# Constant operand rows filled on chip, operand parts stored as they are made, later slot zeroing, a loop written out, and weight tiles of two experts, in a transformer and mixture-of-experts kernel

## The chip, the core and the metric

The kernel runs on one core of a Trainium2 chip. Its engines are TensorE (PE, with a weight load PEld that overlaps the matmuls), VectorE (DVE), ScalarE (ACT), GpSimd (POOL) and SyncE (SP, which here only issues DMAs). A "q" behind an engine's name (SPq, PEldq) is its sequencer: the part that reads instructions, computes registers, waits on semaphores and issues DMAs. The metric is the device time of one execution in microseconds, lower is better.

## The reference

The input x has 2 batches of 512 tokens of 128 values. Two layers follow, each `x = x + ffn(cond(x))`:

- Layer 0, cond: attention of 16 heads of 8 values. Q, K and V come from x by `c_attn_w` and `c_attn_b`; a key and a value of an image row (from `cond_1024`, `uk`, `uv`) stand ahead of the 512 others; the scores are causal, an additive mask row is added, softmax, then the values and `c_proj`.
- Layer 0, ffn: eight experts; each token goes to the two with the highest score and takes the mean of their outputs. An expert is 128 to 512 (W1), gelu, 512 to 512 (W2), gelu, 512 to 128 (W3).
- Layer 1, cond: a product with a weight that `cond_1024` scales and norms. Layer 1, ffn: a two-matrix expert layer with top-2 routing and a capacity of 320 tokens an expert.

## The kernel before

**Attention operands.** Scores are made in bf16 with the precision of float32: Q and K are each cut into three bf16 parts (high, middle, low), and the products that matter are summed over six rows per head dimension, 48 rows in all. Three rows more carry the mask (ones in Q, mask parts in K) and three the negated row maximum (maxima in Q, ones in K). ACT and DVE make the parts of Q and K of a batch `b` into `part` (lines 743, 745, 1285, 1291). SP stores them in DRAM as `q_rows[b]` and `k_rows[b]`, [64 rows, 16 heads, tokens], one DMA for each group of 8 rows (`store_parts`, L463), beside ten DMAs of constant rows (L472 to L480, from `mrowone` and `mrowzero`) and six of mask rows (L485). Then it loads them back by groups of four heads into one of four slots of `qr` and `kr` (`load_rows`, L500 and L501), which POOL has filled with zeros (L639). Everything of this stands in the order of SP's queue: constants, mask, parts of batch 0, loads of groups 0 and 1, parts of batch 1, loads of groups 2 and 3, maxima.

**Attention.** There are eight groups n (two batches of four). A first pass (`score`, L948 and L950, and the reduction L1416 on DVE) gives the row maxima; DVE copies them, transposed, to `mrow` (L1427), and SP puts them in `qr` (`store_max`, L507). A second pass (`second_scores`, L962 and L968) gives exponents (ACT, L784), and `values` (L990) the outputs. An order written out by hand (`schedule`) merges the first pass of group n with the second pass of group n - 2, so the second pass of group 0 comes right after the first two score pieces of group 2.

**Expert weights of layer 0.** 24 tiles of 512 KB go through a ring of four (`w_ring`, loads issued by POOL, L645); ACT makes the high f16 part (`high_part`, L760), DVE the low one (`low_part`, L1357). They stand at fixed places of the schedule: nine sparse, the rest two score units apart near its end. A W2 tile is 128 rows by 128 columns of all eight experts, so its runs in DRAM are 512 bytes. `x0_slots` (4.1 MB), `x1_slots` and `y_rows` (2.3 MB) are zeroed by four DMAs of ACT's queue (L736), whose source is a zeroed weight buffer.

**Expert layer 0.** 23 blocks of 128 tokens. Block i on PE: `second_layer(i)` (12 matmuls of 512 columns, L1093), `first_layer(i+2)` (L1081), `transpose_x(i+3)` (L1070), `transpose_z(i)` (L1104), `third_layer(i-1)` (L1115). ACT has `gelu1(i+2)` and `gelu2(i)` (L796), DVE the copies and splits, SP the loads of tokens. The expert of a block is a value in a table in SBUF; `table` (L412) loads it into registers of an engine (TENSOR_LOAD). Three blocks are written out, then four iterations of a loop of four blocks (`Fori`, L1139 on PE) with one load for seven values on PE (six on ACT, four on DVE and SP), then four blocks written out again with one load. Layer 1 follows.

## Time and profile before

| | us |
|---|---|
| three runs: median (lowest to highest) | 462.86 (460.72 to 464.38) |
| the profiled execution | 464.21 |
| its span | 462.4 |
| mean granted clock of PE, as a share of 2.4 GHz | 0.828 |

| engine | busy us | share of the span | instructions |
|---|---|---|---|
| PE | 313.4 | 68% | 2480 |
| PEld | 189.5 | 41% | 2495 |
| DVE | 282.1 | 61% | 719 |
| ACT | 176.4 | 38% | 405 |
| POOL | 135.5 | 29% | 161 |

The span is one execution on the chip. Busy shares are averages over stages with different limits: which engine or DMA ends the wait in a stage has to be read there. "issue" as a releaser means that the engine waited for nothing that the profile shows, so its own sequencer was late. By stage: operands of attention 0 to 50 us, attention to 204, routing and transition to 225, the blocks of expert layer 0 to 352, layer 1 to the end.

### The profile page before, as it was taken

The page shows a single profiled execution, that of the slowest core. Times are in us where ns is not written, and L with a number is a line of the kernel's source. Part 1 is how long each engine was busy: PE and PEld are TensorE (multiplying, and loading weights), DVE is VectorE, ACT ScalarE, POOL GpSimd, SP SyncE. Part 2 cuts the span into 40 slices and gives each one's busy share as a digit, 9 for nine tenths or more (in the row PEclk, how much of TensorE's full clock was granted, in tenths as well). Part 3 has the DMA queues.
Part 4 walks back from the last instruction along what each step waited for, and adds up shares of the span by engine and source line. Part 5 has one row for each costly group of instructions (what it writes and reads, how often), then busy time and mean ns, then how long its engine had stood idle before and what let it go on. Part 6 is the DMA issues. An engine that isn't in the chain of part 4 may idle for free.

```text
span 462.4 us, 8035 instructions
## 1 busy us (share of the span) xinstructions
PE 313.4 (68%) x2480; PEld 189.5 (41%) x2495; DVE 282.1 (61%) x719; ACT 176.4 (38%) x405; POOL 135.5 (29%) x161
## 2 busy tenths in 40 slices
PE   4550447999987777446579797989894436577820
PEld 2440223444444322225256555645552423365620
DVE  4870463888887755356875656655666683474623
...
GB/s 264 291 212 146 233 251 29 50 130 127 118 74 53 15 232 265 100 41 47 119 83 180 130 21 24 23 28 17 23 13 12 98 29 51 69 30 62 38 43 139
DMA packets 24802, 45.21 MB, mean 98 GB/s; under 512 B 4098, under 2 KB 14930, under 8 KB 24644
## 3 DMA queue, kind: packets, MB, share of 16 engines
...
## 4 chain that ended last, share of the span: by engine, by line
PE 42%; DVE 15%; issue 13%; DMA 10%; SPq 10%; another core or an unknown queue 5%; ACT 3%; POOL 2%; ACTq 0%; DVEq 0%; POOLq 0%
PE pair L1093 15%; PE bank L990 4%; SPq L463 3%; DMA k_rows<-part 3%; PE bank L1104 3%; PE bank L968 2%; PE bank L1115 2%; DMA w_ring<-in_L_ffn_W_dram 2%; PE pair L1081 2%; PE pair L948 2%; DMA qr<-mrow 2%; PE bank L982 2%; SPq L485 2%; DMA back<-y_rows 2%
## 5 line engine op out<-in xcount | busy, mean ns | idle before, releaser
L1093 PE MATMUL pair<-w_sb,h 128*128 x276 | 68.1, 400 | 16.5 <-issue 9.4
L1416 DVE TENSOR_REDUCE mA<-pair 128x2 f32<-128x256 f32 (+3 forms) x64 | 50.9, 820 | 36.9 <-PE pair L950 36.3
L645 POOL DMA_DIRECT2D w_ring<-in_L_ffn_W_dram x24 | 21.5, 897 | 140.8 <-DVE w_sb L1357 108.7
L796 ACT ACTIVATE h<-pair,cols 128x128 f32<-128x128 f32 x92 | 26.2, 368 | 92.2 <-PE pair L1081 70.9
L784 ACT ACTIVATE p_ring<-bank 128x512 f32<-128x512 f32 (+1 forms) x88 | 45.9, 562 | 34.5 <-PE bank L971 34.4
L948 PE MATMUL pair<-kr,qr 128*128 128x128 bf16 (+3 forms) x122 | 32.8, 323 | 25.5 <-DMA kr<-k_rows 21.0
...
L1093 PEld LDWEIGHTS pair<-w_sb,h 128*128 128x128 f16 x276 | 26.3, 102 | 49.6 <-issue 23.9
L660 POOL DMA_INDIRECT x_slots<-sent,slot x32 | 31.1, 971 | 40.1 <-DVE slot L1671 16.7
L968 PE MATMUL bank<-qr,kr 128*128 128x384 bf16 (+3 forms) x120 | 33.4, 322 | 5.8 <-ACT p_ring L784 5.6
L948 PEld LDWEIGHTS pair<-kr,qr 128*128 128x128 bf16 x128 | 13.2, 105 | 47.8 <-issue 31.3
L1357 DVE SCALAR_TENSOR_TENSOR w_sb<-w_ring,w_sb 128x1024 f16<-128x1024 f32 x22 | 26.7, 1219 | 7.4 <-ACT w_sb L760 7.3
L1530 DVE COPY z<-pair 128x512 f32<-128x512 f32 x23 | 15.9, 691 | 24.6 <-PE pair L1093 24.6
L796 ACT ACTIVATE h<-bank,cols 128x128 f32<-128x128 f32 x92 | 26.6, 394 | 7.2 <-PE bank L1104 7.2
L950 PE MATMUL pair<-causal_a,identb 128*128 128x128 bf16 x128 | 27.7, 235 | 1.1 <-DVE mA L1416 0.8
L760 ACT ACTIVATE w_sb<-w_ring 128x1024 f16<-128x1024 f32 x22 | 23.2, 1057 | 12.5 <-PE pair L1022 9.6
L971 PE MATMUL bank<-causal_b,identb 128*128 128x128 bf16 x128 | 26.3, 232 | 1.1 <-issue 0.8
L990 PE MATMUL bank<-p_ring,v_sb 128*9 128x512 f32 (+3 forms) x256 | 24.7, 459 | 0.7 <-ACT p_ring L784 0.5
L1230 PE MATMUL bank<-w_sb,hT 128*128 128x128 f16 (+1 forms) x288 | 20.9, 229 | 4.8 <-issue 3.2
L777 ACT ACTIVATE pimg<-bank 128x512 f32<-128x512 f32 x8 | 4.8, 598 | 47.2 <-PE bank L962 47.2
L968 PEld LDWEIGHTS bank<-qr,kr 128*128 128x128 bf16 x128 | 13.0, 102 | 23.2 <-ACT p_ring L784 12.0
L1230 PEld LDWEIGHTS bank<-w_sb,hT 128*128 128x128 f16 (+1 forms) x288 | 18.2, 107 | 8.5 <-issue 4.4
...
## 6 DMA issues: line engine op xcount, KB each, us to landing
...
```

The lines of the kernel that those rows point to most:

```text
L660: pool.indirect_dma_start(dst, bass.IndirectOffsetOnAxis(ap=slots[:, k, b, r:r + 1], axis=0), row.bitcast(F16) if dst is x0_d else row, No ...
L784: act.activation(p_ring[:, w % P_RING, 0:width], bank(4 + v % 3)[:, 0:width], ACT.Exp).then_inc(exp_done, 1)
L796: ins = act.activation(to[:, c * P:(c + 1) * P], got[:, c * P:(c + 1) * P], ACT.Gelu, bias=cols[:, bass.ds(e * HC + (bias_row + c), 1)], s ...
L948: mm(to[:, 0:n_keys], qr[:, n % SLOTS, j, t * P:(t + 1) * P], kr[:, n % SLOTS, j, IMG:IMG + n_keys], start=True, stop=False)
L950: ins = mm(to[:, t * P:n_keys], identb[:, :], causal_a[:, :], start=False, stop=True)
L968: mm(to[:, i * width:(i + 1) * width], kr[:, n % SLOTS, j0 + i, IMG + kc * P:IMG + (kc + 1) * P], qr[:, n % SLOTS, j0 + i, kc * P:], start ...
L971: ins = mm(to[:, i * width:i * width + P], identb[:, :], causal_b[:, :], start=False, stop=True, skip_group_check=True)
L990: ins = mm(bank(7)[32 * j:32 * j + HD + 1, kc * P:], v_sb[:, b, kc, g * G + j, :], p_ring[:, w % P_RING, i * width:(i + 1) * width], start ...
L1093: ins = mm(bank(3), h1[:, s, hq, k * P:(k + 1) * P], w2_sb[k][wq][:, bass.ds(e * HID, HID)], start=(k == 0 and n == 0), stop=(k == HC - 1 ...
L1230: ins = mm(bank(4 + e % 2)[0:k, t * P:t * P + D], hT[:, e % 2, hq, c, t * P:t * P + k], cp16[wq][:, e, c * D:(c + 1) * D], start=(c == 0 a ...
L1357: dve.scalar_tensor_tensor(out=lo, in0=w_ring[n % W_RING][:, :, :], scalar=W_UP, in1=hi, op0=ALU.mult, op1=ALU.subtract).then_inc(w_lo, 1)
L1416: dve.tensor_reduce(mA[:, b, t, g * G + 2 * hp:g * G + 2 * hp + 2], got[:, :, 0:(t + 1) * P], AX_X, ALU.max).then_inc(a_used, 1)
```

## The change

- The constant rows are no longer stored in DRAM and loaded again. ACT fills all of `qr` and `kr` (an activation of a zero column with a bias that holds ones in rows 64 to 66 or 96 to 98); POOL clears a few columns of `kr` behind it. The mask parts go straight to `kr`. DRAM keeps 48 rows, and a slot's load has 48 rows. For groups 4 to 7, whose slots are used again, SP issues four DMAs more for each (three of mask, one of zero maxima).
- Head channels are put in the order (dimension, head), by ACT copies of the weight columns (`wqk`) and of three rows (`rows_own`), so that a stored part is one DMA over all partitions; each part is stored as soon as it is made, in copies, three DMAs each for Q and K of a batch instead of six. PE waits for both copies (`wqk_ready`, `own_ready`).
- Seven small loads move from ACT's queue to SP's. The zeroing of `x0_slots` moves from ACT's queue to POOL's, behind the first four weight tiles. That of the other two stands behind ACT's fills.
- W2 and W1 tiles are two experts by 128 rows by 512 columns: runs of 2048 bytes. W3 is as before.
- The blocks of expert layer 0 are written out; each engine loads one value a block. PE has 19 loads instead of 6, ACT 19 instead of 6, DVE 21 instead of 5, SP 20 instead of 5.

The core of the diff (names and renamed arguments that only follow are left out):

```diff
-Q_PART = (0, 0, 1, 1, 0, 2)
-K_PART = (0, 1, 0, 1, 2, 0)
-PROD_ROWS = len(Q_PART) * HD
-MASK_ROW = PROD_ROWS
-MAX_ROW = MASK_ROW + 3
-ZERO_ROW = MAX_ROW + 3
-ROWS = 64
+Q_PART = (0, 0, 0, 1, 1, 2)
+K_PART = (0, 1, 2, 0, 1, 0)
+ROWS = len(Q_PART) * HD
+MASK_ROW = 64
+MAX_ROW = 96
 SLOTS = 4
+ONES2 = 1.0 + 16256 / 2 ** 23
...
+            k, two = divmod(n, HC)
+            pair_of = slice(2 * two, 2 * two + 2)
+            in_pair = lambda t: t[:, 2 * two * HID:(2 * two + 2) * HID]
             if n < HC * HC:
-                k, m = divmod(n, HC)
-                return W2[:, cols_of(k), cols_of(m)], [by_expert(t, cols_of(m)) for t in w2_sb[k]]
-            k = (n - HC * HC) % HC
+                return (W2[pair_of, k * P:(k + 1) * P, :].rearrange("e p n -> p e n"),
+                        [in_pair(t) for t in w2_sb[k]])
             if n < HC * HC + HC:
-                return W1[:, :, cols_of(k)], [by_expert(t, cols_of(0)) for t in w1_sb[k]]
-            return W3[:, cols_of(k), :], [by_expert(t, cols_of(0)) for t in w3_sb[k]]
+                return W1[pair_of].rearrange("e p n -> p e n"), [in_pair(t) for t in w1_all]
+            k = two
+            return W3[:, k * P:(k + 1) * P, :].rearrange("e p n -> p e n"), [t[:, :] for t in w3_sb[k]]
...
+            for to, source, signal in (
+                    (vb_bc[:, :], attn_b[2 * D:3 * D].partition_broadcast(P), misc_in),
...
+                    rows = (k_rows_d if i else q_rows_d)[b].rearrange("(c d) h t -> (d h) c t", d=HD)
+                    width = IMG + S if i else S
+
+                    def store(first, last, m, copies):
+                        src = part[:, n, m:m + last - first, 0:width] if copies == 1 else (
+                            part[:, n, m:m + 1, 0:width].broadcast_to([P, copies, width]))
+                        sp.dma_start(rows[:, first:last], src).then_inc(rows_out[n], 16)
+
+                    sp.wait_ge(hi_ready, n + 1)
+                    store(*((5, 6, 0, 1) if i else (0, 3, 0, 3)))
+                    sp.wait_ge(act_step, n + 1)
+                    store(*((3, 5, 0, 1) if i else (3, 5, 1, 2)))
                     sp.wait_ge(parts_ready, n + 1)
-                    rows, which = (k_rows_d[b], K_PART) if i else (q_rows_d[b], Q_PART)
-                    width = IMG + S if i else S
-                    for c, m in enumerate(which):
-                        sp.dma_start(rows[c * HD:(c + 1) * HD].rearrange("d h t -> h d t"),
-                                     part[:, n, m, 0:width]).then_inc(rows_out[n], 16)
...
-                sp.dma_start(k_rows_d[b][MASK_ROW:MAX_ROW, :, 0:IMG].rearrange("r h t -> h r t"),
-                             zero_rows_of(3, IMG)).then_inc(krest_out[b], 16)
-            sp.wait_ge(mask_ready, 1)
-            for b in range(B):
+                    store(*((0, 3, 0, 1) if i else (5, 6, 2, 1)))
+
+            def load_mask(b, first, last, signal):
+
                 for m in range(3):
-                    sp.dma_start(k_rows_d[b][MASK_ROW + m:MASK_ROW + m + 1, :, IMG:],
-                                 mpart[b:b + 1, m:m + 1, :].broadcast_to([1, H, S])
-                                 ).then_inc(krest_out[b], 16)
+                    sp.dma_start(kr[MASK_ROW + m:MASK_ROW + m + 1, first:last, :, IMG:].rearrange("p s j t -> p (s j) t"),
+                                 mpart[b:b + 1, m:m + 1, :].broadcast_to([1, (last - first) * G, S])
+                                 ).then_inc(signal, 16)
...
                 if n >= SLOTS:
                     sp.wait_ge(s_done, s_index(n - SLOTS + 1, 0))
+                    load_mask(b, n % SLOTS, n % SLOTS + 1, qk_in[n % SLOTS])
+                    sp.dma_start(qr[MAX_ROW:MAX_ROW + 3, n % SLOTS],
+                                 zero_row[:, :].rearrange("p (o t) -> p o t", o=1).broadcast_to([3, G, S])
+                                 ).then_inc(qk_in[n % SLOTS], 16)
...
             store_parts(0)
+            sp.wait_ge(filled, 2)
+            sp.wait_ge(trimmed, 1)
+            sp.wait_ge(mask_ready, 1)
+            load_mask(0, 0, SLOTS, masked)
             rows_stored(0)
-            sp.wait_ge(padded, 1)
             load_rows(0)
             load_rows(1)
...
-            for t in (qr, kr):
-                ins = pool.memset(t[:, :, :, :].bitcast(U32), 0)
-            ins.then_inc(padded, 1)
+            pool.wait_ge(filled, 2)
+            pool.memset(kr[MAX_ROW:MAX_ROW + 3, :, :, 1:IMG], 0.0).then_inc(trimmed, 1)
...
             pool.wait_ge(qk_in[1], 32)
             for n in range(W_RING):
                 load_weights(n)
+            x0_clear = x0_d.rearrange("(h p n w) c -> h p n (w c)", h=2, p=P, w=CLEAR_RUN)
+            run = CLEAR_RUN * (2 * D + 2)
+            for h in range(2):
+                pool.dma_start(x0_clear[h], zeros[:, 0:run].rearrange("p (o c) -> p o c", o=1).broadcast_to(
+                    [P, x0_clear.shape[2], run])).then_inc(zero0_out, 16)
...
+            act.wait_ge(fill_ready, 1)
+            for t, col in ((qr, 1), (kr, 2)):
+                flat = t[:, :, :, :].rearrange("p s j t -> p (s j t)").bitcast(F32)
+                act.activation(flat, fill[:, 0:1].broadcast_to([P, flat.shape[1]]), ACT.Identity,
+                               bias=fill[:, col:col + 1]).then_inc(filled, 1)
+                if col == 1:
+                    act.wait_ge(wqkv_in, 16)
+                    act.copy(wqk[:, :, :].rearrange("p i (d h) -> p i d h", h=H),
+                             wqkv[:, 0:2 * D].rearrange("p (i h d) -> p i d h", i=2, d=HD)).then_inc(wqk_ready, 1)
+            act.wait_ge(rows_in, 16 * 9)
+            own = slice(ROW_QK, ROW_UK + 1)
+            act.copy(rows_own[own, :].rearrange("p (d h) -> p d h", h=H), by_dim(rows_sb[own, :])).then_inc(own_ready, 1)
+
             x1_clear = x1_d[0:DUMP1].rearrange("(p n w) d -> p n (w d)", p=P, n=4)
             y1_clear = y1_d[1:FREE1].rearrange("(p n w) d -> p n (w d)", p=P, n=1)
             act.wait_ge(zeroed, 1)
             act.wait_ge(x_in, 16)
-            for target in (x0_clear[0], x0_clear[1], x1_clear, y1_clear):
+            for target in (x1_clear, y1_clear):
...
+            own = slice(ROW_QK, ROW_UK + 1)
+            pe.wait_ge(own_ready, 1)
+            tr(bank(2)[:, own], rows_own[own, :], ident[own, own])
             tr(bank(2)[:, P:2 * P], uk_sb, ident[:, :])
             tr(bank(2)[:, 2 * P:3 * P], uv_sb, ident[:, :]).then_inc(cols_done, 1)
             pe.wait_ge(xT_ready, 1)
-            pe.wait_ge(wqkv_in, 16)
-            mm(bank(4), wqkv[:, 0:D], xT[:, 0, :], start=True, stop=True).then_inc(qkv_done, 1)
-            mm(bank(5), wqkv[:, D:2 * D], xT[:, 0, :], start=True, stop=True).then_inc(qkv_done, 1)
+            pe.wait_ge(wqk_ready, 1)
...
+            first_layer(1, 1)
             pe.wait_ge(tab_ready, 1)
-            of = table(mybir.EngineType.PE, 0, 0, LEAD + 2)
-            for i in range(LEAD):
-                second_layer(0, i, of[i])
-                first_layer(0, i + 2, of[i + 2])
-                transpose_x(0, i + 3)
-                transpose_z(0, i)
+            of = list(table(mybir.EngineType.PE, 0, 0, LEAD + 2))
+            for i in range(NB):
+                second_layer(i, of[i])
+                if i + 3 < NB and i + 3 >= len(of):
+                    of += table(mybir.EngineType.PE, 0, i + 3, 1)
+                if i + 2 < NB:
+                    first_layer(i + 2, of[i + 2])
+                if i + 3 < NB:
+                    transpose_x(i + 3)
+                transpose_z(i)
                 if i == 0:
                     pe.wait_ge(w_lo, W_TILES - W3_POOL)
                     pe.wait_ge(w_lo_pool, W3_POOL)
                 if i:
-                    third_layer(0, i - 1, of[i - 1])
-            with pe.Fori(0, LOOPS) as j:
-                of = table(mybir.EngineType.PE, 0, UNROLL * j + (LEAD - 1), UNROLL + 3)
-                for n in range(UNROLL):
-                    second_layer(j, LEAD + n, of[n + 1])
-                    first_layer(j, LEAD + n + 2, of[n + 3])
-                    transpose_x(j, LEAD + n + 3)
-                    transpose_z(j, LEAD + n)
-                    third_layer(j, LEAD + n - 1, of[n])
-            of = table(mybir.EngineType.PE, 0, REST - 1, NB - REST + 1)
-            for i in range(REST, NB):
-                second_layer(0, i, of[i + 1 - REST])
-                if i + 2 < NB:
-                    first_layer(0, i + 2, of[i + 3 - REST])
-                if i + 3 < NB:
-                    transpose_x(0, i + 3)
-                transpose_z(0, i)
-                third_layer(0, i - 1, of[i - REST])
-            third_layer(0, NB - 1, of[NB - REST])
+                    third_layer(i - 1, of[i - 1])
+            third_layer(NB - 1, of[NB - 1])
...
+            of = list(range(LEAD - 1))
+            for i in range(NB):
+                if i == LEAD - 1:
+                    dve.wait_ge(lead_in, 16 * LEAD)
+                    copy(id_all[:, LEAD - 1:LEAD], xg_lead[:, LEAD - 1, 2 * D:].bitcast(I32)).then_inc(id_copied, 1)
+                    dve.wait_ge(id_copied, 1)
+                copy_z(i)
+                if i >= len(of):
+                    of += table(mybir.EngineType.DVE, 0, i, 1)
+                if i + 3 < NB:
+                    copy_x(i + 3)
+                if i + 2 < NB:
+                    split_1(i + 2)
```

**SP's queue where the operands of batch 0 are stored.** Before, between the second batch's constants and the load of group 0 (`part` is the cut operand, `mpart` the cut mask):

```order
L472 DMA q_rows<-mrowone 16x3x512
L474 DMA q_rows<-mrowzero 16x13x512
L476 DMA k_rows<-mrowone 16x3x544
L478 DMA k_rows<-mrowzero 16x10x544
L480 DMA k_rows<-mrowzero 16x3x32
L485 DMA k_rows<-mpart 16x1x512 x6
L463 DMA q_rows<-part 16x8x512 x6
L463 DMA k_rows<-part 16x8x544 x6
L500 DMA qr<-q_rows 64x2048
L501 DMA kr<-k_rows 64x2176
```

and in the changed program, from the last small input load on:

```order
L461 DMA gate_sb<-in_L_ffn_gate_w_dram 128x8
L473 DMA q_rows<-part 128x3x512
L473 DMA q_rows<-part 128x2x512
L473 DMA q_rows<-part 128x512
L473 DMA k_rows<-part 128x544
L473 DMA k_rows<-part 128x2x544
L473 DMA k_rows<-part 128x3x544
L485 DMA kr<-mpart 1x16x512 x3
L503 DMA qr<-q_rows 48x2048
L504 DMA kr<-k_rows 48x2176
```

28 DMAs (ten constants, six of mask, twelve parts) stood ahead of the first load of a slot; now nine do.

**ACT's start in the changed program** (before, ten input loads and four zeroing DMAs stood ahead of its first cast):

```order
L725 DMA wqkv<-in_L_cond_c_attn_w_dram 128x384
L726 DMA uk<-in_L_cond_uk_w_dram 128x128
L727 DMA uv<-in_L_cond_uv_w_dram 128x128
L732 ACT_TABLE_LOAD
L732 ACTIVATE qr<-fill 128x4096
L736 COPY wqk<-wqkv 128x256
L732 ACTIVATE kr<-fill 128x4352
L740 COPY rows_own<-rows_sb 3x128
L748 DMA x_slots<-w_sb 512x1x645
L748 DMA y_rows<-w_sb 128x2048
L756 CAST part<-q 128x512
```

Both fills stand ahead of the copy that PE waits for.

**PE in the blocks of expert layer 0.** Before, at the start of an iteration of four blocks:

```order
L1115 MATMUL bank<-w_sb,h 128x128
L1139 UNCONDITIONAL_BRANCH
L1139 ISA
L412 TENSOR_LOAD tab
L1088 REGISTER_ALU
L1090 REGISTER_ALU
L1093 ISA
L1093 MATMUL pair<-w_sb,h 128x512 x2
```

Now, in every block from the third to the twentieth (L1105 is `second_layer`, L1093 `first_layer`):

```order
L1105 REGISTER_ALU
L1105 MATMUL pair<-w_sb,h 128x512
L409 TENSOR_LOAD tab
L1093 ISA
L1093 MATMUL pair<-xgT,w_sb 128x128 x2
```

The load has moved from behind the short matmuls of `third_layer` to behind the long ones of `second_layer`, and has one value instead of seven.

## Rows read from the trace of the kernel before

**Rows 1.** The chain of waits, 0 to 51 us: start us, us, what.
```profile
16.69 2.33 SPq L472
...
42.69 2.44 DMA k_rows<-part
```

**Rows 2.** The timeline, 0 to 48 us: start us, us, engine, operation, [idle before <-releaser].
```profile
9.18 1.92 PE L897 MATMUL bank<-xT,wqkv 128*128 128x512 f32 x2
...
13.89 3.50 POOL L639 MEMSET qr<- 128x4096 uint32 x1
...
15.08 6.02 DVE L1304 TENSOR_SCALAR kimg_bd<-hmask,k 128x16 f32<-128x16 f32 x2
...
21.29 0.73 DVE L1273 TENSOR_SCALAR q<-bank,cols 128x512 f32<-128x512 f32 x1
...
34.00 0.42 DVE L1350 COPY wcT_sb<-pair 128x256 f32<-128x256 f32 x1 [0.58 <-PE pair L932]
...
45.72 0.60 SPq L501 DMA_DIRECT2D kr<-k_rows  x1
```

**Rows 3.** Groups of ACT instructions with shapes: count, busy us, mean ns, idle before.
```profile
L760 ACT ACTIVATE w_sb<-w_ring 128x1024 f16<-128x1024 f32 x22 | 23.2, 1057 | 12.5 <-PE pair L1022 9.6 <-DMA w_ring<-in_L_ffn_W_dram 2.8
...
L743 ACT ACT_TABLE_LOAD x1 | 1.3, 1283 | 10.3 <-issue 10.3
```

**Rows 4.** The timeline, 50 to 74 us.
```profile
50.50 0.26 PE L948 MATMUL pair<-kr,qr 128*128 128x128 bf16 x1 [16.54 <-DMA kr<-k_rows]
...
61.40 0.41 DVE L1427 COPY mrow<-pair 12x512 bf16<-12x512 bf16 x1
...
69.46 0.27 PE L948 MATMUL pair<-kr,qr 128*128 128x128 bf16 x1 [4.43 <-DMA kr<-k_rows]
...
73.08 0.62 PE L962 MATMUL bank<-qr,kr 128*32 128x512 bf16 x4 [3.03 <-DMA qr<-mrow]
```

**Rows 5.** The chain of waits, 65 to 73 us.
```profile
65.78 7.25 DMA qr<-mrow
```

**Rows 6.** Stretches: busy us (x) of PE, PEld, DVE, ACT, POOL; PEclk, DMA share, GB/s.
```profile
12.00:30.00 18.00, 9.97 (x48) 8.04 (x47) 15.27 (x27) 4.67 (x8) 8.91 (x5) 0.72 1.02 292
56.00:70.00 14.00, 7.05 (x44) 3.45 (x44) 9.72 (x18) 0.00 (x0) 1.04 (x2) 0.79 1.00 229
```

**Rows 7.** Who waited for whom, 140 to 225 us: us, times, longest.
```profile
ACT w_sb L760 <- DMA w_ring<-in_L_ffn_W_dram: 2.8, 2, 2.6
```

**Rows 8.** The chain of waits, 257 to 333 us.
```profile
257.33 2.68 PE pair L1093 x12
...
271.01 2.76 PE pair L1093 x12
...
275.88 2.72 PE pair L1093 x12
...
326.01 2.68 PE pair L1093 x12
...
332.30 2.76 PE pair L1093 x12
```

**Rows 9.** Single instructions of lines 412 and 1076: count, ns min/median/max, first start us.
```profile
L412 PEldq TENSOR_LOAD <-tab x1: 777/777/777, 224.0 to 224.0; - x1
...
L412 PEldq TENSOR_LOAD <-tab x1: 1711/1711/1711, 262.4 to 262.4; - x1
...
L412 ACTq TENSOR_LOAD <-tab x1: 908/908/908, 330.7 to 330.7; - x1
...
L1076 PEldq ALU_OP  x1: 32/32/32, 258.1 to 258.1; - x1
```

**Rows 10.** A stretch behind a loop boundary; columns as in Rows 6.
```profile
264.50:269.20 4.70, 4.70 (x21) 2.12 (x21) 0.29 (x1) 0.00 (x0) 0.81 (x1) 0.64 0.04 14
```

**Rows 11.** The timeline, one PE and one ACT row of the loop.
```profile
264.47 4.31 PE L1093 MATMUL pair<-w_sb,h 128*128 x12 [2.35 <-issue]
...
330.51 1.16 ACT L796 ACTIVATE h<-bank,cols 128x128 f32<-128x128 f32 x4
```

273 lines of the change are left out of this document (114 added, 159 removed).

## The prediction

> **What bounds the kernel now.** I went from the page's strip of 40 slices, which shows PE nearly idle in the first tenth, to the chain of waits. From 10 to 43 us it is one thing: SP issuing DMAs, each constant taking some 2.3 us to issue, and then the last stored part landing 2.44 us after its issue [rows 1]. SP and not the data is late: Q of batch 1 is computed at 21.3 us, and the last result that PE needs for its first score is copied at 34.0 to 34.4 us [rows 2]. Yet the first score starts at 50.50 us, after 16.54 us of idle time that a load of `kr` ends. Then PE works for 14.5 us, waits 4.43 us for the slot of group 2 and, two score pieces on, 3.03 us for the maxima of group 0, so the second pass starts at 73.08 us [rows 4]. Those maxima were ready at 61.8 us; the last of their DMAs took 7.25 us to land [rows 5], in a stretch in which the DMA engines were busy all the time at 229 GB/s [rows 6]. From there to the end of attention PE leads, but for 2.8 us that ACT waits for weight tiles [rows 7]. In the expert blocks PE leads too: a block takes 275.88 - 271.01 = 4.87 us [rows 8].
>
> **The first score.** The sum is against the profiled execution, 464.2 us, which is 1.3 us over the median shown; I leave that difference alone.
>
> ACT now starts with a table load of 1.28 us and two fills. From 1.06 us for 1024 elements [rows 3] 4096 and 4352 elements are an estimated 3.6 to 4.2 and 3.8 to 4.5 us. With the three DMA issues ahead (to about 2.3 us) and the two copies (0.7 us together) PE gets `rows_own` at about 12.5 us; behind it stand three transposes, so the first QK matmul starts near 13.1 us instead of 9.18 [rows 2]: 3.9 us later. Against that, POOL's fills go. Two products of 16 columns took 6.02 us on DVE while POOL filled `qr` and `kr` [rows 2]; the work behind them slipped from an estimated 17.6 us (their plain lengths added) to 21.29 us, 3.7 us. The two cancel to +0.2 us: PE is ready near 34.7 us.
>
> The other path is SP's. The last part of K of batch 0 is made at about 23.3 us (22.7 us before, the same shifts). Its store covers three copies: 1 us of issue and, from 2.44 us for a third of its bytes, 3 to 4 us of landing: 27 to 28 us; three mask DMAs lie beside it. The load of group 0 then took from 45.72 to 50.50 us, 4.8 us [rows 2, 4]: 33.5 us. Or by traffic: 2.3 MB of zeroing and 1.6 MB of parts at 229 to 292 GB/s [rows 6] are 13 to 17 us from 13 us on, thus 26 to 30, and the load at 31 to 36. I take 36 us for the first score, the later end, since the zeroing overlaps the stores. It cannot be before 34.7. The upper bound is that SP goes on issuing at 2.3 us each: nine DMAs from 16.6 us are 37.3, two loads 42, and with landing 44.5 us.
>
> **The second pass.** From the first score, PE needs 14.5 + 0.6 = 15.1 us of work to the second pass, thus 51.1 us. The maxima are ready 11.3 us after the first score, as before: 47.3 us; three issues at 0.6 us [rows 2], then landing, between 2.44 us [rows 1] and 7.25 us [rows 5]: 51.5 to 56.4 us. What speaks for the upper end is that 4.1 MB of zeroing now stand on POOL's queue right behind 2 MB of weights; against it, that before the maxima stood behind 1 MB of slot loads in their own queue, which now are 0.8 MB and issued some 12 us ahead of them. I take 53.5 us: **-19.6 us**, between -23 (49.9, all at its best) and -9 (44.5 + 15.1, and 4 us for the maxima).
>
> SP's four further DMAs for each of groups 4 to 7 cost 2.4 us of its queue, at 0.6 us each; a slot is free a group of work (12 us, nearly all of it PE's) ahead of its use and its load took 4.8, so they lie beside PE's work: 0, and if that cover were gone 4 x 2.4 us. POOL's clearing of a few columns of `kr` and the moved input loads lie ahead of 16 us on queues that wait: 0.
>
> **Weight tiles.** The runs of 2 KB can shorten a load; ACT's and DVE's part has the same 1024 elements, and its pace of two exponents and one high part (1.9 us a tile) sets the dense stretch. So at most the 2.8 us of [rows 7] is to be had, at least nothing: **-1.5 us**.
>
> **The blocks.** A loop boundary takes 264.47 - 257.33 = 7.14 us instead of 4.87 [rows 8, 11]: 2.27 us, four times; the boundary at the loop's exit 332.30 - 326.01 = 6.29, thus 1.42 [rows 8]. Together **-10.5 us**. PE's idle time there is marked as its own issue [rows 11], and the register load fills it: 1.71 us for seven values [rows 9]. Behind this boundary the granted clock was 0.64 of full speed, thus mostly the lower of the two levels, 1.2 GHz [rows 10]; the block took 271.01 - 264.47 = 6.54 us, 1.67 over, and one more behind another boundary about the same. These I count as gone with the idle time that precedes them: **-3.5 us**, at worst 0.
>
> What is added is a load in 18 blocks. At 258.1 us PE's sequencer had issued all of `second_layer` and was at the next register operation [rows 9], while those matmuls ran until 257.33 + 2.68 = 260.01 us [rows 8]: it is 1.9 us ahead. The new load stands in exactly this place. Its length for one value no row shows; five values on an idle PE took 0.78 us, seven 1.71 [rows 9], so I take 0.8 us as the nearest and 1.71 as the bound. With some 0.3 us of waits and register operations behind it, 1.1 us is hidden and even 1.9 nearly. That a load runs beside queued work is seen on ACT: one of 0.91 us from 330.7 [rows 9] while four activations ran from 330.51 to 331.67 us [rows 11]. ACT's `gelu2` may start 0.4 us later; what it feeds has over 1 us to spare. I add **+1 us** in all for such remains.
>
> The DMA page of the Trainium skill ("DMA: Bandwidth & Descriptors", section "Latency and other measured facts") speaks against this part: it gives a register load a floor of some 600 ns and says that the compiler unrolls by four to spread it. By that rule alone, all loads exposed, the time would be that of the second rival; the trace's 0.78 us for five values agrees with the floor, and only the place decides.
>
> **Sum.** 464.2 - 19.6 - 1.5 - 10.5 - 3.5 + 1.0 = 430.1: I predict **430 us**, with 422 to 437 for this case by itself.
>
> **The rivals.**
>
> 1. *The DMAs stay late.* SP's issues stay slow while the zeroing runs, or the maxima sit behind it; the second pass starts at 60 to 64 us and the gain is 9 to 13 instead of 19.6. For it: three small DMAs took 7.25 us under such traffic [rows 5]; against: two thirds of the zeroing is gone from that time. 437 to 441 us. Chance 0.14.
> 2. *The register loads are exposed*, on PE or by way of ACT or DVE: 18 x 0.6 to 0.8 us is 11 to 14 us, less the 1 us counted: 440 to 443 us. Against it stands the run-ahead of 1.9 us. Chance 0.12. Both together, about 452 us: 0.03.
> 3. *Slower than before*: PE's load waits until the array is empty and each block pays what a boundary paid. PE idled 2.35 us there [rows 11]; 18 times is 42 us, and the low clock behind two of five such gaps adds 18 x 0.4 x 1.7 = 12 us: 430.1 - 1 + 54 = 483 us. It makes the kernel slower from (464.2 - 429) / 18 = 2.0 us a block on. Against it: one value instead of seven and no branch. Chance 0.04.
> 4. *No difference*: the earlier start is given back in attention, since maxima, weights and slot loads share DMA queues with 4.1 MB more in that time, and the blocks win only part. Attention's 131 us from the second pass on would have to grow by 15 us or more; PE leads there. About 460 us, chance 0.03.
> 5. *More than summed*: the first score at 34.7 us and PE at the high clock level near attention's end. 415 to 421 us, chance 0.03.
>
> **The numbers.** The forecast has 0.61. The range 419 to 446 us leaves out rivals 3 to 5 and half of the double case, and part of the forecast's own spread, which makes 2 in 10 by a generous count of what I can't see. A measurement of this kernel can tell about 1% (4.6 us) from no change. Faster by more: the forecast, rivals 1, 2, 5 and the double case, 0.93. Within: 0.03. Slower: 0.04.
>
> **What would show it.** The first score at 35 to 37 us, its wait ended by a load of `kr` or by the copy of `wcT`, no DVE instruction of 6 us near 15 to 21 us; the second pass at 51 to 56 us; the first QK matmul near 13 us; blocks of 4.8 to 5.0 us throughout with no gap on PE before `first_layer`, and loads of 0.6 to 0.9 us; the blocks in about 114 instead of 127 us. The prediction is wrong if the maxima land after 57 us, if PE idles behind each load, or if the clock level falls inside the blocks.

## The result, and the profile after

| | before | after |
|---|---|---|
| median of the runs of this comparison (lowest to highest), us | 463.62 (460.72 to 467.16) | 426.06 (418.98 to 427.67) |
| ratio, 95% interval | | 0.909 (0.894 to 0.924) |
| the profiled execution, its span, us | 464.21, 462.4 | 418.98, 417.2 |

The change makes the kernel 8 to 9% faster; 430 us were forecast, with a range of 419 to 446. Ratios, here and below, are of the runs within 1.5% of the fastest of their kernel (418.98 and 424.34 us of six runs of the changed one), and the medians of the table alone would give 0.919. The profiled execution of the changed kernel is the shortest of its runs, 7 us under the median, so a sum over its stages gives more than the medians do. Its granted clock was 0.870, that of the other five 0.840 to 0.847.

The first reading is the start. These are rows of the changed kernel's timeline, the answer to [rows 2, 4] (start, length, engine, line and operation, idle time before and what ended it):

```profile
12.17 0.26 PE L902 MATMUL pair<-ident,rows_own 3*128 3x3 f32 x1 [4.23 <-ACT rows_own L740]
...
12.84 1.92 PE L907 MATMUL bank<-xT,wqk 128*128 128x512 f32 x2
...
18.17 0.37 DVE L1304 TENSOR_SCALAR kimg_bd<-head_of,k 128x16 f32<-128x16 f32 x2
...
25.03 0.42 SPq L504 DMA_DIRECT2D kr<-k_rows  x1
...
31.60 3.13 POOL L648 DMA_DIRECT2D w_ring<-in_L_ffn_W_dram  x4 [17.92 <-DMA kr<-k_rows]
...
33.41 0.42 DVE L1350 COPY wcT_sb<-pair 128x256 f32<-128x256 f32 x1 [0.59 <-PE pair L942]
...
34.07 0.27 PE L960 MATMUL pair<-kr,qr 128*128 128x128 bf16 x1 [0.70 <-issue]
...
51.79 0.40 PE L974 MATMUL bank<-qr,kr 128*32 128x512 bf16 x4 [2.43 <-DMA qr<-mrow]
```

PE waits 4.23 us for the copy of three rows that stands behind ACT's fill of `kr`. The two products that took 6.02 us on DVE beside POOL's fills take 0.37. Before, five DVE instructions that began between 15.08 and 17.09 us all ended between 21.09 and 21.37, when POOL's second fill ended (21.05): they stood still more than they ran slowly. SP issues the load of `kr` for group 0 at 25.03 us instead of 45.72, and POOL's row at 31.60 shows a load of `kr` as landed (it waits for group 1). The first score starts 0.66 us after the copy of `wcT` does, and its releaser is "issue", no load: the preparation on PE and DVE is late now, SP is not. It comes at 34.07 us instead of 50.50, and the second pass at 51.79 instead of 73.08. Of what still stands before that one, the chain of waits says:

```profile
46.98 4.76 DMA qr<-mrow
```

This answers to the 7.25 us of [rows 5]. And the stretches that answer to [rows 6] (us, then busy us of PE, PEld, DVE, ACT and POOL, the granted clock, DMA share, GB/s):

```profile
12.00:30.00 18.00, 12.67 (x57) 9.56 (x57) 12.98 (x32) 5.47 (x10) 1.63 (x2) 0.88 0.71 203
36.00:50.00 14.00, 9.18 (x61) 4.24 (x59) 12.73 (x22) 0.00 (x0) 0.23 (x1) 0.88 1.02 319
```

From 12 to 30 us the DMA engines now move 203 GB/s instead of 292; from 36 to 50 us they are full at 319 GB/s, with weights and the zeroing of `x0_slots` beside the maxima.

The second reading is the blocks. The chain of waits has `second_layer` of three blocks in a row, and one register load of PE follows it in the view of its line (count, ns least, median, most, first and last start):

```profile
242.67 2.71 PE pair L1105 x12
...
247.49 2.65 PE pair L1105 x12
...
252.25 2.69 PE pair L1105 x12
```

```profile
L409 PEldq TENSOR_LOAD <-tab x1: 301/301/301, 243.5 to 243.5; - x1
```

From the third on, a block takes 4.76 to 4.89 us, 4.80 in the mean; the load of one value takes 0.30 us, and no idle time stands behind it. Boundaries of 7.14 us [rows 8, 11] are gone, and so is the lower clock behind them [rows 10]. In the first two blocks it is not: `second_layer` takes 4.17 us in block 0 of this profile and 4.64 in block 1 of the second one.

Two pairs of profiles by stage, in us; "again" is a second profile of each kernel, from two later jobs in which the kernel before takes 452 and 454 us:

| stage, from the start of | before | after | before, again | after, again |
|---|---|---|---|---|
| the program, to the second pass | 73.08 | 51.79 | 71.99 | 53.10 |
| the second pass, to group 7 | 97.67 | 96.23 | 98.28 | 95.76 |
| group 7, to the first block | 54.45 | 45.44 | 42.81 | 40.49 |
| the first block, to the last `third_layer`'s end | 129.55 | 114.39 | 137.74 | 119.14 |
| layer 1, to the end | 107.70 | 109.38 | 98.06 | 99.32 |
| span | 462.4 | 417.2 | 448.9 | 407.8 |

The border at the first block is a soft one. Where that block starts early, PE waits in block 0, for its first tokens and for DVE: in the changed kernel the first block starts at 193.46 and 189.35 us, the third at 204.11 and 204.56.

### The profile page after: what moved, and what is told of

The parts are those of the page before. It is cut to its first block, busy times and chain, and to the rows that moved or that the text cites. A ratio compares the mean times of both kernels' runs of the same rounds, so it can differ in the third digit from the quotient of the medians.

```text
span 417.2 us, 7917 instructions
## 1 busy us (share of the span) xinstructions
PE 306.3 (73%) x2495; PEld 188.8 (45%) x2495; DVE 276.5 (66%) x719; ACT 185.4 (44%) x408; POOL 125.7 (30%) x163
## 3 DMA queue, kind: packets, MB, share of 16 engines
q0 software_dynamic: 8336, 26.47, 19.6%
## 4 chain that ended last, share of the span: by engine, by line
PE 55%; DVE 17%; issue 10%; DMA 6%; ACT 6%; POOL 2%; SPq 1%; another core or an unknown queue 1%; ACTq 1%; POOLq 0%; DVEq 0%
PE pair L1105 14%; PE bank L1002 4%; PE bank L1228 4%; PE bank L1115 4%; PE bank L1126 4%; PE pair L960 3%; DVE mA L1416 3%; PE pair L1093 3%; PE bank L980 3%; PE bank L994 2%; PE pair L1216 2%; ACT p_ring L798 2%; DMA y_rows<-y_sb,id_now 2%; POOL y_rows L718 2%; PE pair L1196 2%
## 5 line engine op out<-in xcount | busy, mean ns | idle before, releaser
L1105 PE MATMUL pair<-w_sb,h 128*128 x276 | 64.7, 385 | 3.9 <-DVE h L1539 3.9
L648 POOL DMA_DIRECT2D w_ring<-in_L_ffn_W_dram x24 | 18.3, 762 | 126.2 <-DVE w_sb L1357 108.3
L668 POOL DMA_INDIRECT x_slots<-sent,slot x32 | 31.7, 990 | 34.1 <-DVE slot L1659 17.2
L1105 PEld LDWEIGHTS pair<-w_sb,h 128*128 128x128 f16 x276 | 25.8, 99 | 33.9 <-issue 6.0
L980 PE MATMUL bank<-qr,kr 128*128 128x512 bf16 (+3 forms) x128 | 34.7, 317 | 5.8 <-ACT p_ring L798 5.6
L960 PE MATMUL pair<-kr,qr 128*128 128x128 bf16 (+3 forms) x128 | 33.7, 320 | 6.7 <-DVE mA L1416 5.7
L1228 PE MATMUL bank<-w_sb,hT 128*128 128x128 f16 (+1 forms) x288 | 22.0, 237 | 7.7 <-issue 5.7
L983 PE MATMUL bank<-causal_b,identb 128*128 128x128 bf16 x128 | 25.2, 225 | 0.0
L1710 DVE SCALAR_TENSOR_TENSOR hT<-w_sb,hT 128x640 f16<-128x640 f32 x16 | 13.0, 823 | 17.4 <-ACT hT L876 11.0
L1228 PEld LDWEIGHTS bank<-w_sb,hT 128*128 128x128 f16 (+1 forms) x288 | 19.5, 111 | 10.6 <-issue 6.6
L1002 PE MATMUL bank<-p_ring,v_sb 128*9 128x512 f32 (+3 forms) x256 | 23.8, 444 | 0.1
```

Source lines behind the costliest of these rows:

```text
L668: pool.indirect_dma_start(dst, bass.IndirectOffsetOnAxis(ap=slots[:, k, b, r:r + 1], axis=0), row.bitcast(F16) if dst is x0_d else row, No ...
L960: mm(to[:, 0:n_keys], qr[:, n % SLOTS, j, t * P:(t + 1) * P], kr[:, n % SLOTS, j, IMG:IMG + n_keys], start=True, stop=False)
L980: mm(to[:, i * width:(i + 1) * width], kr[:, n % SLOTS, j0 + i, IMG + kc * P:IMG + (kc + 1) * P], qr[:, n % SLOTS, j0 + i, kc * P:], start ...
L983: ins = mm(to[:, i * width:i * width + P], identb[:, :], causal_b[:, :], start=False, stop=True, skip_group_check=True)
L1002: ins = mm(bank(7)[32 * j:32 * j + HD + 1, kc * P:], v_sb[:, b, kc, g * G + j, :], p_ring[:, w % P_RING, i * width:(i + 1) * width], start ...
L1105: ins = mm(bank(3), h1[:, s, hq, k * P:(k + 1) * P], w2_sb[k][wq][:, bass.ds(e * HID, HID)], start=(k == 0 and n == 0), stop=(k == HC - 1 ...
```

## The experiments

All ratios are to the kernel before, run in the same job on the same chip. The last stage takes 98 to 114 us from profile to profile, mostly by job and not by kernel, so times of two jobs are compared by their ratios alone.

**1. Both kernels again.** No edit.

> The changed kernel once more, nothing edited. Its profiled run took 418.98 us, its other runs 424 to 428 us. Theory A: the difference of some 7 us is PE's granted clock in the last group of attention and the routing behind it (in the profiled run group 7 took 158.0 to 193.5 us with a clock of 0.63 to 0.87, before 170.8 to 225.2), so this profile has a span of 423 to 426 us, the same first score (34 us) and the same start of the second pass (51 to 53 us), blocks of 4.8 us, and 4 to 7 us more between the start of group 7 and the first block. Rival B: the difference is in the early DMAs (the maxima land later), so the second pass starts at 56 us or later. Time 424 to 428 us either way.

Measured: 410.96 us against 452.41, ratio 0.907 (0.901 to 0.913). First score at 34.8 us and second pass at 53.1, as A said; but from group 7 to the first block it took less (40.5 us), not 4 to 7 us more. So A is wrong for this job. Between the two profiles the last stage differs by 10.1 us (table), and what group 7 gains the first two blocks lose. For the 7 us within the first job the clocks on record (0.870 against 0.840 to 0.847) speak for the clock; no other run of that job has a trace, so the place stays open.

> The kernel before once more, for a profile of it beside the others. From the start of group 7 of attention to the third expert block the first profile took 64.6 us (170.75 to 235.35), while five profiles with the blocks written out took 55.7 to 57.7 us. Theory A: the 7 to 9 us are an accident of the first profile (the lower clock in group 7 and a DVE instruction of 4.92 us at 216.99 us), so this profile shows 56 to 59 us there. Rival B: they belong to the kernel with the loop, so this profile shows 63 to 66 us again. Its first score at 50.5 us, its second pass at 71 to 73 us, its loop boundaries 7.1 to 7.3 us either way.

Measured: from group 7 to the third block 58.2 us (170.27 to 228.47), so A. In the first pair this stretch takes 64.6 us before and 56.1 after (8.5 us), in the second 58.2 and 55.7 (2.5 us): most of what the first pair shows there does not come back. Whether it was in the first job's other runs no trace shows. But behind each of the four loop boundaries a block ran slow, not behind two of them:

```profile
258.90 4.45 PE L1093 MATMUL pair<-w_sb,h 128*128 x12 [2.30 <-issue]
...
265.58 2.76 PE L1093 MATMUL pair<-w_sb,h 128*128 x12
```

```profile
258.90:263.40 4.50, 4.50 (x16) 1.80 (x17) 0.05 (x1) 0.00 (x0) 0.89 (x1) 0.62 0.05 15
263.40:267.90 4.50, 4.38 (x41) 2.79 (x38) 3.45 (x9) 2.17 (x8) 0.33 (x1) 1.00 0.05 15
```

The first fence is PE's timeline, the second two stretches of it. The block behind a gap of 2.30 us takes 6.68 us, and its `second_layer` runs at a granted clock of 0.62, so mostly at 1.2 GHz; the next is at full clock.

**2. The blocks written out, and nothing else.** The functions of the expert blocks as in the diff; operands, weights and zeroing as before.

```diff
-            with pe.Fori(0, LOOPS) as j:
...
+            for i in range(NB):
+                second_layer(i, of[i])
+                if i + 3 < NB and i + 3 >= len(of):
+                    of += table(mybir.EngineType.PE, 0, i + 3, 1)
```

> The kernel before with the expert blocks written out, and nothing else of the change. Theory A (the loop's share is what the prediction summed, 10.5 us of boundaries and 3.5 us of clock behind two of them, less 1 us): 449 to 452 us, blocks of 4.8 us, register loads of one value at 0.3 us with no idle time of PE behind them. Rival B (the blocks gained in the change because everything ahead of them was earlier or its weight tiles came sooner): 455 to 460 us. Rival C (more instructions make the start or the code's loading longer): 453 to 456 us, with the first score later than 50.5 us.

Measured: 435.84 us against 452.41, ratio 0.962 (0.958 to 0.966), thus 17 us instead of 13. Blocks are 4.77 to 4.90 us from the third on, and the stage takes 119.7 us against the 137.7 of the second profile of the kernel before: the mechanism is A's, the size is larger, and that profile says why, since four blocks are slow in it and not two. First score at 50.42 us: nothing for C.

**3. The same with the weight tiles of two experts.**

```diff
-                return W2[:, cols_of(k), cols_of(m)], [by_expert(t, cols_of(m)) for t in w2_sb[k]]
+                return (W2[pair_of, k * P:(k + 1) * P, :].rearrange("e p n -> p e n"),
+                        [in_pair(t) for t in w2_sb[k]])
```

> The kernel before with the blocks written out and the weight tiles of two experts (runs of 2048 bytes); operands, constants and zeroing as before. Theory A (the tiles only take away ACT's 2.8 us of waits for tiles): 1 to 3 us under the kernel with the blocks alone, that is 446 to 451 us, and no wait of ACT for a weight tile over 1 us between the sixth and the eighth group. Rival B (the tiles are worth nothing, since ACT and DVE set the pace there): equal within 1 us. Rival C (the 9.9 us that the profiled run of the change gained between the start of group 6 and the first block are the tiles'): 440 to 443 us.

Measured: 430.76 us, ratio 0.952 (0.948 to 0.956), which is 0.010 under that of the blocks alone, or 4.5 us of 452, against the same runs. That is more than A's 1 to 3 us and less than C's. For each kernel follow three rows: its tiles on the DMA page (count, KB, median us to landing), the last of the maxima's DMAs in the chain, and ACT's waits for tiles (us, times, longest). Blocks alone:

```profile
w_ring<-in_L_ffn_W_dram POOLq DMA_DIRECT2D x24, 512.0 KB, 6.1
```

```profile
64.60 6.59 DMA qr<-mrow
```

```profile
ACT w_sb L744 <- DMA w_ring<-in_L_ffn_W_dram: 3.1, 2, 2.6
```

With the tiles:

```profile
w_ring<-in_L_ffn_W_dram POOLq DMA_DIRECT2D x24, 512.0 KB, 4.6
```

```profile
64.43 4.33 DMA qr<-mrow
```

```profile
ACT w_sb L747 <- DMA w_ring<-in_L_ffn_W_dram: 0.6, 2, 0.4
```

ACT's wait goes from 3.1 to 0.6 us, which is the forecast's term. The other half is in a place where I had looked for none: the first four tiles share the DMA engines with the slot loads and the maxima, a tile lands in 4.6 instead of 6.1 us, the maxima in 4.33 instead of 6.59, and the second pass starts at 68.80 instead of 71.24 us. From 56 to 71 us both kernels move 236 GB/s, at a DMA share of 0.93 with the old tiles and 0.80 with the new.

With experiment 1 this makes a ladder within one job: the blocks bring 16.6 us (452.41 to 435.84), the tiles 5.1 (to 430.76), and what remains, the operands and the zeroing, 19.8 (to 410.96).

**4. The copy that PE waits for ahead of the fill of `kr`.**

```diff
+                    act.wait_ge(rows_in, 16 * 9)
+                    own = slice(ROW_QK, ROW_UK + 1)
+                    act.copy(rows_own[own, :].rearrange("p (d h) -> p d h", h=H), by_dim(rows_sb[own, :])).then_inc(own_ready, 1)
-            act.wait_ge(rows_in, 16 * 9)
-            own = slice(ROW_QK, ROW_UK + 1)
-            act.copy(rows_own[own, :].rearrange("p (d h) -> p d h", h=H), by_dim(rows_sb[own, :])).then_inc(own_ready, 1)
```

> The changed kernel with ACT's copy of rows_own ahead of its fill of kr instead of behind it. In the changed kernel PE waited 4.2 us for that copy (its three transposes start at 12.17 us), and the first score at 34.07 us came behind PE's and DVE's preparation, while the load of kr of group 0 had landed at 31.6 us. Theory A (the first score now waits for preparation, which hangs on this copy): first QK matmul near 9.0 us, first score at 31 to 32 us, the second pass 2 to 3 us earlier, 421 to 425 us. Rival B (the stores and loads of the parts do not move with it, or the maxima land at the same time because of weights and zeroing on the queues): the first score is earlier, the second pass not, time as the changed kernel within 1 us. Rival C (kr's fill, now later by 0.4 us, or POOL and DVE in each other's way, holds the mask and the loads back): the first score at 34 us or later.

Measured: 409.87 us, 1.1 us under the changed kernel in the same job (410.96); ratio 0.898 (0.891 to 0.905) against 0.907 (0.901 to 0.913). The intervals overlap, so by time alone no difference is shown. The timeline shows the mechanism of A, more of it than expected:

```profile
7.85 0.42 ACT L740 COPY rows_own<-rows_sb 3x128 f32<-3x128 f32 x1
...
9.00 1.92 PE L907 MATMUL bank<-xT,wqk 128*128 128x512 f32 x2
...
30.87 0.26 PE L960 MATMUL pair<-kr,qr 128*128 128x128 bf16 x1 [0.70 <-issue]
...
48.37 0.40 PE L974 MATMUL bank<-qr,kr 128*32 128x512 bf16 x4 [1.43 <-DMA qr<-mrow]
```

The QK matmul is at 9.00 instead of 12.82 us, the first score at 30.87 instead of 34.79, the second pass at 48.37 instead of 53.10. The later groups start 3.0 to 3.2 us earlier and the first block 2.9 (186.41 against 189.35). The last stage took 103.1 us against 99.3, which hides it in this profile. As the first score moved by what the QK matmul moved (3.9 and 3.8 us), it did hang on the preparation.

**5. Where the zeroing of `x0_slots` stands.** Later than in the change, then as early as before:

```diff
+            pool.wait_ge(max_in[0], 48)
             for h in range(2):
                 pool.dma_start(x0_clear[h],
...
```

> The changed kernel with POOL waiting for the landed maxima of group 0 before it zeroes x0_slots (4.1 MB); one wait is added, nothing else. In the changed kernel the maxima took 4.8 us to land (46.98 to 51.74 us) while weights and zeroing kept the DMA engines busy, and PE idled 2.4 us. Theory A (the maxima land late because of that traffic): they land in 2.0 to 3.0 us, the second pass starts 2 to 2.5 us earlier, 0.994 to 0.996 of the changed kernel's time. Rival B (the length is that of the DMA itself or of three issues one behind the other): it stays within 0.5 us. Rival C (zeroing later collides with the slot loads of groups 4 and 5 or with weight tiles): PE or ACT waits there, time the same or 1 to 3 us longer.

Measured: 409.77 us against 453.95, ratio 0.906 (0.899 to 0.914). The maxima landed by 50.12 us, under 1.5 us behind their last issue, and PE no longer waits:

```profile
46.78 1.94 SPq L510 DMA_DIRECT2D qr<-mrow  x3
...
50.12 1.46 POOL L658 DMA_DIRECT2D x_slots<-w_sb  x2 [14.27 <-DMA qr<-mrow]
...
50.70 0.40 PE L975 MATMUL bank<-qr,kr 128*32 128x512 bf16 x4
```

So A holds for the landing. The gain does not last: the second pass starts 2.4 us earlier than in the changed kernel's second profile (53.10), group 1 only 0.8 us (62.94 against 63.73), group 6 also 0.8. The time is the changed kernel's.

```diff
-            for h in range(2):
-                pool.dma_start(x0_clear[h],
...
+            for h in range(2):
+                act.dma_start(x0_clear[h],
...
             for target in (x1_clear, y1_clear):
```

> The changed kernel with both zeroing DMAs of x0_slots back on ACT's queue, ahead of the other two, so that 6.5 MB are zeroed from 8 us on, as in the kernel before; nine DMAs still stand ahead of the first slot load. Theory A (SP's issues were slow in the kernel before because the zeroing kept the DMA engines busy, so that 28 DMAs took 2.3 us each): the nine DMAs take some 2.3 us each again, the first score comes at 40 to 44 us instead of 34.5, the maxima land faster, the second pass starts 4 to 8 us later; 1.01 to 1.02 of the changed kernel's time. Rival B (the number of DMAs alone made it late): the first score within 1 us of 34.5, the second pass 1 to 2 us earlier because no zeroing stands beside the maxima.

Measured: 411.58 us, ratio 0.909 (0.902 to 0.916). SP's queue of this kernel, and then of the changed one (its second profile):

```profile
24.93 4.73 SPq L485 DMA_DIRECT2D kr<-mpart  x3
30.75 0.33 SPq L503 DMA_DIRECT2D qr<-q_rows  x1
31.13 0.42 SPq L504 DMA_DIRECT2D kr<-k_rows  x1
```

```profile
23.21 1.89 SPq L485 DMA_DIRECT2D kr<-mpart  x3
25.37 0.35 SPq L503 DMA_DIRECT2D qr<-q_rows  x1
25.76 0.42 SPq L504 DMA_DIRECT2D kr<-k_rows  x1
```

Under the zeroing three issues take 4.73 instead of 1.89 us, and the first load is issued 5.4 us later, so A is right on SP's pace (about 1.6 us an issue, not 2.3). But the first score waits only 1.85 us for it and comes at 35.35 us instead of 34.79:

```profile
35.35 0.27 PE L960 MATMUL pair<-kr,qr 128*128 128x128 bf16 x1 [1.85 <-DMA kr<-k_rows]
...
37.89 3.12 POOL L648 DMA_DIRECT2D w_ring<-in_L_ffn_W_dram  x4 [24.20 <-DMA kr<-k_rows]
```

The maxima's last DMA took 4.58 us (4.82 in the changed kernel), though no zeroing of `x0_slots` stood beside it any more. The second row has a reason: POOL waits for group 1's slot load before it issues the weight tiles, so these came 5.6 us later (32.32 us in the changed kernel) and were still under way. The time does not tell the two places of the zeroing apart. So the zeroing's place is worth 0.6 us of the first score; the other 15.6 us (50.95 to 35.35) belong to the rest of the operand part, of which the 28 issues that became nine are the likely bulk. No run takes that part alone.

**6. The register load's place and length.** In the changed kernel, PE's load ahead of `second_layer`:

```diff
+                if i >= LEAD and (i - LEAD) % 4 == 0:
+                    n = min(7, NB - i + 1)
+                    of[i - 1:] = table(mybir.EngineType.PE, 0, i - 1, n)
                 second_layer(i, of[i])
-                if i + 3 < NB and i + 3 >= len(of):
-                    of += table(mybir.EngineType.PE, 0, i + 3, 1)
```

> The changed kernel whose PE loads seven expert numbers at once, ahead of second_layer of blocks 3, 7, 11, 15 and 19 (five numbers at the last), where the loop loaded them, instead of one number in each block behind second_layer; blocks written out, no branch. Theory A (the 2.3 us at a loop boundary are the register load in an exposed place, and the branch costs little): these five blocks take 6.3 to 7.2 us instead of 4.8, together 8 to 12 us more, 1.02 to 1.03 of the changed kernel's time, with some at the lower clock. Rival B (the branch and the refill of instructions behind it cost most of the 2.3 us): the five blocks take 5.0 to 5.8 us, 1 to 5 us in all.

Measured: 418.82 us against 453.95, ratio 0.929 (0.920 to 0.938). The load, and PE's timeline around it:

```profile
L409 PEldq TENSOR_LOAD <-tab x1: 1700/1700/1700, 250.7 to 250.7; - x1
```

```profile
252.68 2.76 PE L1105 MATMUL pair<-w_sb,h 128*128 x12 [1.67 <-DVE h L1540]
...
257.59 2.76 PE L1105 MATMUL pair<-w_sb,h 128*128 x12
```

PE idles 1.67 us behind a load of 1.70 us. The row names DVE's `h`, but that had ended at 252.03 us, and the load only at 252.41. The five blocks take 6.85, 6.54, 6.53, 6.60 and 6.09 us, 8.6 us over 4.80 in all, no slow one behind them: A, but for the lower clock that it also expected. With a load of the same length PE idled 2.1 to 2.4 us at the loop's boundaries, so the branch had a part too: some 0.5 us of each idle time, and, as no block is slow without it, perhaps the fall of the clock.

The same with `min(10, NB - i + 1)`:

> The changed kernel whose PE loads ten expert numbers at once (nine and five at the last two) in the places where it loaded seven in the run before: ahead of second_layer of blocks 3, 7, 11, 15 and 19. Three numbers of each load are not needed; they only make it longer. With seven, PE idled 1.7 us and stayed at 2.4 GHz behind it; at the loop boundaries it idled 2.1 to 2.4 us, and behind four of five in the last profile of the kernel before it ran a block at the lower level, 1.67 to 1.9 us longer. Theory A (the length of the idle time decides, and not the branch): the loads take 2.3 to 2.5 us, PE idles 2.3 us, and at least two of the blocks behind take 6.4 us or more beyond the gap; 1.02 to 1.035 over the changed kernel. Rival B (the branch, with its refill of instructions, decides): no block beyond the gap is over 5.1 us; 1.022 to 1.026.

Measured: 444.25 us against 467.11, ratio 0.950 (0.943 to 0.956). All of PE's loads, and the matmuls behind the four long ones:

```profile
L409 PEldq TENSOR_LOAD <-tab x6: 782/2286/2463, 198.3 to 307.5; - x6
```

```profile
218.50 4.45 PE L1105 MATMUL pair<-w_sb,h 128*128 x12 [2.47 <-issue]
...
241.89 4.43 PE L1105 MATMUL pair<-w_sb,h 128*128 x12 [2.38 <-issue]
...
265.25 2.76 PE L1105 MATMUL pair<-w_sb,h 128*128 x12 [2.42 <-issue]
...
286.80 4.45 PE L1105 MATMUL pair<-w_sb,h 128*128 x12 [2.20 <-issue]
```

Without any branch, gaps of 2.20 to 2.47 us are back, and behind three of four `second_layer` takes 4.43 to 4.45 us instead of 2.76, at the lower level: A, the clock falls behind idle time of this length, and no branch is needed. The length alone does not settle a single case: the clock held behind 2.42 us and fell behind 2.20.

The load of one value behind `third_layer`, in every block:

```diff
+                if LEAD + 2 <= i + 2 < NB:
+                    of += table(mybir.EngineType.PE, 0, i + 2, 1)
                 second_layer(i, of[i])
-                if i + 3 < NB and i + 3 >= len(of):
-                    of += table(mybir.EngineType.PE, 0, i + 3, 1)
```

> The changed kernel whose PE loads its one expert number of a block ahead of second_layer, behind the short matmuls of third_layer, instead of behind second_layer; everything else the same. Seven numbers in this place left PE idle for 1.7 us, with a register load of 1.70 us. Theory A (a load costs its own length where the sequencer has no work queued ahead, and one number takes 0.30 us): blocks of 5.0 to 5.15 us instead of 4.80, 18 of them 4 to 6 us in all, 1.010 to 1.015 of the changed kernel's time. Rival B (0.3 us are covered even there): blocks of 4.80 us, time the same.

Measured: 434.46 us against 467.11, ratio 0.929 (0.923 to 0.935).

```profile
246.07 2.75 PE L1105 MATMUL pair<-w_sb,h 128*128 x12 [0.26 <-issue]
...
251.26 2.75 PE L1105 MATMUL pair<-w_sb,h 128*128 x12 [0.33 <-issue]
```

Blocks take 5.12 to 5.30 us, in 18 blocks together 7 us over 4.80 each, somewhat more than the 4 to 6 of A. The same load costs nothing behind `second_layer`.

By ratios across jobs the three kernels take 1.024, 1.047 and 1.024 of the changed kernel's time, where A had 1.02 to 1.03, 1.02 to 1.035 and 1.010 to 1.015. From the third block to the end of the blocks they took 9.2, 16.3 and 7.3 us more than its 103.9, thus 2.2, 4 and 1.8%: the rest of the last two lies outside the blocks.

**7. POOL's products in the first block.** DVE makes all W3 low parts, three of them behind its copy of `z` of block 0, and PE waits for them a block later.

```diff
-W3_POOL = 2
+W3_POOL = 0
...
+            pool.wait_ge(w_hi, W_TILES)
...
-                if i == 0:
-                    pe.wait_ge(w_lo, W_TILES - W3_POOL)
-                    pe.wait_ge(w_lo_pool, W3_POOL)
+                if i == 1:
+                    pe.wait_ge(w_lo, W_TILES)
...
+                if i == 0:
+                    low_part(W_EARLY + 1)
+                    low_part(W_EARLY + 2)
...
+                if i == 0:
+                    low_part(W_EARLY + 3)
```

> The changed kernel with the low parts of the last two W3 tiles made by DVE instead of POOL, three of DVE's four W3 tiles moved behind its copy of z of block 0, and PE's wait for them moved from block 0 to just ahead of third_layer of block 0. In the changed kernel block 0 and 1 take 8.6 and 6.6 us instead of 4.8; POOL's two products of 2.7 us (188.9 to 194.3 us) lie beside DVE instructions of 2.82 us instead of 1.22 and of 2.34 us instead of 0.42. Theory A (DVE is slowed by POOL's products, and PE waits for DVE): blocks 0 and 1 take 5 to 6.5 us each, 2 to 4 us in all, 0.991 to 0.995 of the changed kernel's time. Rival B (PE waits there for the first tokens of block 3, which land at 194.2 us): block 0 stays over 7 us, gain under 1 us.

Measured: 425.25 us against 467.11, ratio 0.912 (0.905 to 0.918), where the changed kernel has 0.907 in another job: no gain. The slowed DVE instructions of the changed kernel are real (second profile, beside POOL's L683 from 188.90 to 194.26 us):

```profile
189.46 2.82 DVE L1357 SCALAR_TENSOR_TENSOR w_sb<-w_ring,w_sb 128x1024 f16<-128x1024 f32 x1
192.20 2.34 DVE L1537 TENSOR_SCALAR h<-h 128x512 f16<-128x512 f32 x1
```

In block 0 the changed kernel (same profile) waits 1.36 us for tokens, as B said, and 2.63 us for DVE's `z`. Here block 0 takes 6.1 us, but block 1 now 7.1, where PE waits 2.35 us for DVE's next `z`; and `second_layer` of block 0 ran at the lower clock, as in the two kernels of experiment 6 from the same job:

```profile
195.59:200.20 4.61, 4.61 (x12) 1.68 (x13) 2.35 (x4) 1.09 (x4) 0.00 (x0) 0.55 0.61 159
```

A names a stall that is there and a gain that is not. The third block starts at 208.84 us, in those two kernels, which up to there are the changed one, at 209.58 and 211.10.

**8. Edits 4, 5 (later) and 7 together.**

> Three edits of the changed kernel together: the copy of rows_own ahead of the fill of kr, the zeroing of x0_slots behind the landed maxima of group 0, and the W3 tiles as in the run before (all low parts on DVE, behind the copy of z, PE's wait later). Theory A (they lie in three stages that follow one another, so their gains add: 4.5, 0.8 and 2 to 4 us): 0.975 to 0.985 of the changed kernel's time, second pass at 46 to 48 us. Rival B (each gain is caught by the next wait, most of all the second pass by the maxima and the zeroing): 0.99 to 1.0.

Measured: 418.05 us against 467.11 in six runs, ratio 0.898 (0.893 to 0.903). The changed kernel's ratio, from another job, was 0.907 (0.901 to 0.913). The second pass starts at 46.47 us. In its own job its ratio is 1.5% under that of the kernel of experiment 7 (0.912), which differs by edits 4 and 5 alone, and the intervals do not meet. It beats the kernel before for certain; over the changed kernel the 1% rests on ratios of two jobs whose intervals overlap by 0.002. By these, 0.898 / 0.907 is 0.990, at the edge of B, and edit 4 alone had the same 0.898: edit 5 loses 1.6 of its 2.4 us within one group, and edit 7 gives nothing.

## Why the prediction was right, and where it was off

- **The first score** (36 us, not before 34.7): 34.07. The QK matmul was put at 13.1 us and came at 12.84. I took the DMA path as the later one; the loads of groups 0 and 1 had both landed by 31.6 us, where I had group 0's at 33.5 to 36, and preparation set the start. Preparation itself was 0.6 us earlier than the floor I gave it: I read the 6.02 us on DVE as two slow products, but five instructions stood still there until POOL's fill ended. That half of rival 5 came true in both profiles (34.79 us in the second); its other half, the high clock near attention's end, shows in the first alone (from the second pass of group 7 on, 148 to 167 us, the granted clock was 0.96; in the second profile, from 149 to 167, it was 0.81).
- **The second pass** (-19.6 us, at 53.5): -21.3 in the first pair of profiles, -18.9 in the second. The landing of the maxima was put between 2.44 and 7.25 us and took 4.76. The size was met with some luck: I had put nothing of the tiles here, and in experiment 3 they bring 2.4 us of it. From that experiment's kernel to the changed one the second pass moves by 15.7 us (68.80 to 53.10), less than forecast, the second pass of group 1 by 17.4, and the time by 19.8. Rival 1 did not come: the second pass was not at 60 to 64 us, and with the zeroing put back in front it came no later (52.72 us). In small both its halves are there: SP's issues up to the masks took 0.6 to 1.5 us each, and PE idled 2.43 us for the maxima beside the traffic.
- **Weight tiles** (-1.5 us): mis-sized. The step "at most the 2.8 us of ACT's waits is to be had" left out that the first four tiles share the DMA engines with slot loads and maxima. Experiment 3 measured 4.5 us by the ratios (5.1 by the medians), of which the second pass's start had 2.4.
- **The loop's boundaries** (-10.5 us) held: PE idled 2.1 to 2.4 us there in both profiles, and 1.5 at the exit. The load did not fill all of it: without the branch a load of the same length left PE idle for 1.7 to 1.9 us. **The clock** (-3.5 us) was mis-sized: the first profile happened to have two slow blocks of four possible, the second had four, and the stage gained 15.2 us in one pair and 18.6 in the other. The slow blocks follow the idle time, as I had counted them; but one profile gave their number. The sign of being wrong that I had named, a fall of the clock inside the blocks, was met in the first two blocks in both profiles; the kernel before has such a slow `second_layer` there too (4.11 and 3.90 us), so little was lost by it.
- **The loads** (+1.0 us, rivals 2 and 3): they cost 0. One value takes 0.30 us, where I had taken 0.8 from the row of five. Both rivals would have needed the other place: there 18 loads cost 7 us (experiment 6). The rule of the Trainium skill that I had weighed ("DMA: Bandwidth & Descriptors", "Latency and other measured facts": a floor of some 600 ns for a register load) disagrees with this trace, whose loads of one value take 0.27 to 0.30 us; the measurement decides.
- **No difference** (rival 4): attention did not grow, it took 1.4 and 2.5 us less from the second pass to group 7, although 4.1 MB more were written in it.

The sum was -34.1 us; the medians moved by 37.6, the second pair of profiles by 41.1. By the ladder of experiment 3 the terms were 19.8 us where 19.6 were forecast, 5.1 where 1.5, and 16.6 where 13 (10.5 + 3.5 - 1): the tiles were mis-sized by 3 to 4 us, clock and loads together by about 4, and both errors had one sign.

What stays open is where the first job's profile of the changed kernel gained its 7 us on its other runs, why the last stage differs by up to 15 us, and how the 19.8 us of the operand part divide among fewer issues, earlier stores, POOL's fills gone and the zeroing moved.
